# A vision tower on one core: new slots, orders and banks for a planned pipeline, with filler matmuls

## The chip, the cores and the metric

The kernel runs on one core of one Trainium2 chip. Its time is the device time in microseconds (us) of one execution. The engines are PE (TensorE), DVE (VectorE), ACT (ScalarE), POOL (GpSimd) and SP (SyncE, which issues all DMAs here). Each takes its instructions strictly in program order.

## What is computed

64 images (3x224x224) are cut into 196 tokens of 256 numbers each. Then come four blocks, each with a residual and a layer norm:

```python
h = tok(x)                                    # 16x16 patches @ W + b
h = ln(h + attn0(h)); h = ln(h + ffn0(h))     # level 0
h = ln(h + attn1(h)); h = ln(h + ffn1(h))     # level 1
# attn0: xz = h @ in_proj; xb = silu(conv4(xb)); dt, B, C = split(xb @ x_proj)
#   dt = softplus(dt * dt_w + dt_b); dA = exp(dt * A)        (512 x 16 states)
#   state[t] = dA[t] * state[t-1] + (xb * dt)[t] * B[t]      (scan over tokens)
#   y = sum_n state * C + xb * D; out = (ln(y) * silu(z)) @ out_w
# ffn0: r = sigmoid(mix(h) @ W_r); k = relu(mix(h) @ W_k)^2; r * (k @ W_v)
# attn1: 8 heads, leaky scores, softmax over 196 tokens, * gamma + x
# ffn1: 8 experts, top 2 by a softmax gate, weighted sum of x @ We + be
```

Everything is float32.

## The kernel before

One image takes 16 **groups** in the scan of attn0: 4 channel blocks of 128 by 4 sets of 4 states. The program is cut into **slots**; one slot holds one group, and an image has 16. Every other block of an image has a slot number of its own in the tables at the top (`AT_...`), counted from the image's first scan: from -41 (load the image) to 89 (store its result). So in each of the 16 slots (slot number modulo 16) the engines work on up to nine images at once. `schedule` writes the program out image by image; `step` in each engine's part goes through the slots, and within a slot the order of its `for s, q in at(...)` lines is the order of that engine's work. Engines meet only through semaphores.

For group g of an image:

- POOL, `inputs` (L464): X = u * B, in slot g-1. X is a ring of six tiles.
- ACT, `decay` (L873): four exponentials into a ring of two dA tiles, in slot g-1.
- DVE, `scan_group` (L1070): two scans over X, in slot g.
- POOL, `times_c` (L474): X = X * C, in slot g+1.
- PE, `sum_states` (L579): transposes X and adds up the states in PSUM bank YB, in slot g+2. ACT empties YB once in four groups (`drain_y`, L880).

The work around the scan that the prediction speaks of:

- `softplus` (L854, L859, L862) in four pieces on ACT: relu, abs, exp, log. The log needs another activation table, so it is followed by a reload ahead of the next `decay`. POOL then adds (dt, L451) and multiplies (u, L454) for the next image: `make_u`.
- `inverse_std` (L479 to L486): four or two small POOL instructions per layer norm ("att", "y", "ffn", "out", "moe"), which wait for `moments` (L1075, L1079) on DVE.
- ffn0: `token_major(.., "r")` and `mix_keys` on PE (L619, L627), `drain_rk` on ACT (rs L915, ka L920), the square on POOL (ka L504), then `token_major(.., "v")`. The first of these needs a PSUM bank that DVE's `add_residual` (accT, L1195) gives free.
- `project_out` on PE (L600, L603) after POOL's y3 product (L511); then `queries_keys` (L636), `drain_qk` (L927, L929), and DVE's `gate_x` (L1055) after ACT's `tanh_of_x` (L828).
- ffn1: DVE's `scale_pair` (hg, L1186) makes one of four pairs of experts at a time in a ring of two tiles; PE's `expert_pair` (L699) uses it.
- attn1: `scores`, `drain_scores` (L937), `row_max` (L1117), `probs` (L944), `turn_probs` (L658), `drain_pT` (L952), `mix_values` (L671), `attended` (L1129 to L1134). Before, the slots of the drains, maxima and exponentials are tied to those of the matmuls: `AT_SCORES[n] + 1`, `+ 2`, `+ 3`, `AT_TURN_P[n] + 1`, `AT_AV[n] + 1`.

Three PSUM banks (G0, G1, G2) are shared by tables of uses; a use can start when the use before it in the same bank has been drained.

Of the kernel before, what the change touches and what calls it, by code (L numbers as in the profile page):

```python
# [11 lines left out]
P = 128  # L12
# [5 lines left out]
T = SIDE * SIDE  # L18
BLK = 2
# [38 lines left out]
AT_LOAD = -41  # L58
AT_PATCH = (-30, -30, -26,)
# [13 lines left out]
AT_SOFT = (-9, -9, -8, -8,)  # L73
AT_U = -7
AT_B = (-2, -4, -1, 0,)
AT_C = (-1, -2, 0, 0,)
AT_Y_OUT = (6, 9, 12, 17,)
# [3 lines left out]
AT_Y_STD = 20  # L81
# [3 lines left out]
AT_Y3 = 24  # L85
# [5 lines left out]
AT_H1T_OUT = 30  # L91
# [22 lines left out]
AT_H3T_OUT = 64  # L114
# [3 lines left out]
AT_TOP2 = 68  # L118
# [66 lines left out]
def vit_tower(nc, x, w_tok, b_tok, w_in, conv_w, conv_b, w_xproj, a_log, d_par, dt_w, dt_b, w_out, ln_g, ln_b,  # L185
              w_r, w_k, w_v, mu_r, mu_k, w_qk, b_q, b_k, w_vv, b_v, gamma, w_g, b_g, w_e, b_e,
              ident, q_mask, k_mask, rank_of, proj, gates, out):
    with ExitStack() as ctx:
# [183 lines left out]
        def _(sp):  # L372
# [40 lines left out]
            def step(b, par):  # L413
                for g in range(GROUPS):
                    def at(slot):
                        return live(b, par, g, slot)

                    for s, q in at(AT_LOAD):
                        load(s)
                    for s, q in at(AT_GATE_STORE):  # L420
                        store_gates(s)
# [24 lines left out]
        def _(pool):  # L446
# [41 lines left out]
            def step(b, par):  # L488
                for g in range(GROUPS):
# [857 lines left out]
```

## Time and profile before

| what | value |
|---|---|
| median of 3 runs | 5539.83 us |
| lowest, highest | 5514.9, 5540.97 us |
| the profiled execution | 5522.53 us, span of the core 5520.7 us |
| busy: PE, DVE, ACT, POOL | 86%, 68%, 71%, 81% of the span |
| mean granted TensorE clock | 0.917 of full speed |

The span begins with the loads of the weights and the first images, whose first scan starts after about 77 us, and ends with 185 us in which the last images pass through the blocks behind the scan. Between them lie 63 steps from image to image, nearly all alike. Busy shares are means over a whole step: in one slot an engine may be the one that all wait for, and in the next have nothing to do.

### The profile page before, as it was taken

Reading aid. Unit: us, or ns where it says so; the run is one execution under the profiler, and the core shown is the slowest. Engines: PE = TensorE matmul, PEld = TensorE weight load, DVE = VectorE, ACT = ScalarE, POOL = GpSimd, SP = SyncE. Lnnn points to the kernel's source line nnn. Section 1 sums busy time; section 2 is a strip of 40 time slices with the busy share of each in tenths; the row PEclk is TensorE's granted clock in tenths of the full one; section 3 lists DMA queues with packets and bytes.
Section 4 is the critical chain, followed back from the end, with each engine's and each line's share of the span. In section 5 each row is a group of like instructions: output and inputs, shape, how many; then the busy total and the mean of one; then the engine's idle time right before and its main releaser. Section 6 shows DMA issues by size and latency. Waiting matters only on the chain.

```text
span 5520.7 us, 91938 instructions
## 1 busy us (share of the span) xinstructions
PE 4738.8 (86%) x31488; PEld 4137.2 (75%) x31488; DVE 3737.4 (68%) x7504; ACT 3925.5 (71%) x9282; POOL 4455.6 (81%) x3336
## 2 busy tenths in 40 slices
PE   4788889888888888888888888888888888888887
PEld 3677777777777777777777777777777777777776
DVE  3667666667677667667677677676776776766663
ACT  4777777777777777776777777777776777776752
POOL 4988888888888888888888888888888888887860
PEclk7889989999999999999999999999999999999887
DMA  4222222222222222222222222222222222222110
GB/s 105 63 47 60 68 55 56 71 50 61 67 54 61 66 56 61 61 60 61 55 67 61 55 64 64 55 62 66 55 62 66 55 58 69 55 57 70 41 39 24
DMA packets 730609, 328.76 MB, mean 60 GB/s; under 512 B 631543, under 2 KB 655393, under 8 KB 729889
## 3 DMA queue, kind: packets, MB, share of 16 engines
q1 hardware_dynamic: 730144, 322.89, 24.0%
q8 instruction: 252, 4.13, 0.3%
q14 instruction: 213, 1.74, 0.1%
HBM read 307.88 MB, written 14.90 MB: 58 GB/s over the span
## 4 chain that ended last, share of the span: by engine, by line
DVE 35%; PE 26%; ACT 26%; issue 9%; POOL 3%; SPq 1%; DMA 0%; DVEq 0%; ACTq 0%; POOLq 0%
DVE X L1070 14%; PE G L699 8%; ACT dA L873 6%; PE YB L579 4%; DVE xbs L1047 3%; DVE nmx L1117 3%; PE SB L658 3%; PE G L619 2%; PE G L671 2%; ACT dt L854 2%; ACT soft L854 2%; ACT y L888 2%; DVE hg L1186 2%; ACT pT L952 2%; ACT pr L937 2%
## 5 line engine op out<-in xcount | busy, mean ns | idle before, releaser
L1070 DVE TENSOR_TENSOR_SCAN X<-dA,X 128x392 f32<-128x392 f32 x2048 | 1875.7, 958 | 1203.7 <-ACT dA L873 1165.0
L474 POOL TENSOR_TENSOR X<-X,Cb 128x784 f32<-128x784 f32 x1024 | 1894.7, 1850 | 4.2 <-DVE X L1070 4.2
L464 POOL TENSOR_TENSOR X<-u,Bb 128x784 f32<-128x784 f32 x1024 | 1895.3, 1851 | 2.2 <-DMA Bb<-proj_rows 2.1
L873 ACT ACTIVATE dA<-dt,negA 128x195 f32<-128x195 f32 x4096 | 1524.0, 417 | 303.3 <-DVE X L1070 263.5
L579 PE MATMUL YB<-idn,X 128*98 128x128 f32 x8192 | 1152.7, 289 | 33.3 <-POOL X L474 33.3
L579 PEld LDWEIGHTS YB<-idn,X 128*98 128x98 f32 x8192 | 973.6, 136 | 138.4 <-POOL X L474 116.8
L699 PE MATMUL G<-hg,we 128*128 128x196 f32 x4096 | 771.9, 348 | 49.8 <-DVE hg L1186 49.6
L699 PEld LDWEIGHTS G<-hg,we 128*128 128x128 f32 x4096 | 730.3, 203 | 61.1 <-issue 58.4
L556 PE MATMUL SB<-hT,win 128*128 128x196 f32 x2048 | 454.9, 386 | 184.2 <-ACT pT L952 170.6
L556 PEld LDWEIGHTS SB<-hT,win 128*128 128x128 f32 x2048 | 415.4, 226 | 214.0 <-ACT hT L808 192.3
L671 PE MATMUL G<-vs,pT 98*98 98x33 f32 x4096 | 428.0, 262 | 130.7 <-DVE att L1134 113.0
L671 PEld LDWEIGHTS G<-vs,pT 98*98 98x98 f32 x4096 | 419.2, 181 | 160.2 <-issue 158.0
L880 ACT ACTIVATE ysb<-YB 98x256 f32<-98x256 f32 x256 | 96.5, 377 | 584.0 <-PE YB L579 540.8
L944 ACT ACTIVATE pr<-pr,nmx 98x196 f32<-98x196 f32 x1024 | 385.0, 450 | 106.6 <-DVE nmx L1117 96.1
L648 PE MATMUL SB<-km,qm 32*98 32x392 f32 x1024 | 255.5, 540 | 169.3 <-DVE xbs L1055 159.5
L1047 DVE SCALAR_TENSOR_TENSOR xbs<-SB,cw,xbs 128x195 f32<-128x195 f32 (+2 forms) x768 | 268.1, 411 | 174.4 <-ACT xbs L817 170.4
L479 POOL TENSOR_TENSOR veps_att<-mv_att,epsc 98x2 f32<-98x2 f32 x64 | 12.5, 195 | 459.0 <-DVE mv_att L1079 459.0
L451 POOL TENSOR_TENSOR dt<-dt,soft 128x784 f32<-128x784 f32 x64 | 117.7, 1839 | 261.6 <-ACT soft L862 261.6
L952 ACT ACTIVATE pT<-SB 98x784 f32<-98x784 f32 x256 | 209.7, 819 | 150.5 <-PE SB L658 114.1
L1186 DVE TENSOR_TENSOR hg<-G,Gb 128x784 f32<-128x784 f32 x256 | 240.5, 961 | 101.7 <-PE G L699 98.3
L547 PE MATMUL G<-patT,wtok 128*128 128x196 f32 x1536 | 275.9, 337 | 11.6 <-ACT patT L799 11.1
L658 PE MATMUL SB<-idn,pr 98*98 98x98 f32 x2048 | 260.8, 279 | 20.3 <-DVE zs L1060 8.7
(147 smaller groups left out, 7379.4 us busy)
## 6 DMA issues: line engine op xcount, KB each, us to landing
Bb<-proj_rows SPq DMA_DIRECT2D x256, 392.0 KB, 4.4
Cb<-proj_rows SPq DMA_DIRECT2D x256, 392.0 KB, 3.8
Gb<-gate_rows SPq DMA_DIRECT2D x64, 784.0 KB, 4.7
px<-in_x SPq DMA_DIRECT2D x1024, 36.8 KB
out<-ob SPq DMA_DIRECT2D x64, 196.0 KB
dtin<-proj_rows SPq DMA_DIRECT2D x64, 98.0 KB, 2.8
we<-in_w_e SPq DMA_DIRECT2D x1, 2048.0 KB
proj_rows<-pj SPq DMA_DIRECT2D x64, 25.3 KB
```

The lines of the kernel that those rows point to most:

```text
L464: tt(X[(GROUPS * s + g) % RING][:], u[q % 2][:, c:c + 1, :].broadcast_to([P, NG, T]), Bb[:, NG * ng:NG * (ng + 1), :], ALU.mult).then_inc( ...
L474: tt(t[:], t[:], Cb[:, n0:n0 + NG, :], ALU.mult).then_inc(prod_ready, 1)
L556: last = mm(o[:, j // 2, (j % 2) * T:(j % 2 + 1) * T], lhsT=win[:, k, m * P:(m + 1) * P], rhs=src[:, k, :], start=(k == 0), stop=(k == DC ...
L579: last = mm(YB[0:TB, k * P:(k + 1) * P], lhsT=X[(GROUPS * s + g) % RING][:, j, k * TB:(k + 1) * TB], rhs=idn[:], is_transpose=True, start= ...
L658: last = nc.tensor.transpose(o[0:TB, j // 2, at:at + TB], pr[(UNITS * s + n) % PRING][:, j, k * TB:(k + 1) * TB], idn[:TB, :TB])
L671: last = mm(o[0:TB, j * (DV + 1):(j + 1) * (DV + 1)], lhsT=pT[:, j // 2, at:at + TB], rhs=vs[q % 2][:, k, h0 + j, :], start=(k == 0), stop ...
L699: last = mm(o[:, m * T:(m + 1) * T], lhsT=we[:, k, at:at + P], rhs=hg[p % GRING][:, e, k, :], start=(p == 0 and e == 0 and k == 0 and m == 0),
L873: last = go(dA[i % DRING][:, j, 1:T], dt_[q % 2][:, c, 1:T], ACT.Exp, scale=negA[:, c, n:n + 1])
L944: last = go(pr[i % PRING][:, j, :], pr[i % PRING][:, j, :], ACT.Exp, bias=nmx[i % PRING][:, j:j + 1])
L1047: last = v.scalar_tensor_tensor(out=xbs[:, c, k:], in0=S.tile[:, c // 2, at:at + T - k], scalar=cw[:, c, TAPS - 1 - k:TAPS - k], in1=xbs[: ...
L1070: v.tensor_tensor_scan(t, dA[i % DRING].rearrange("p n t -> p (n t)"), t, 0.0, ALU.mult, ALU.add).then_inc(scan_done, 1)
L1186: v.tensor_tensor(hg[p % GRING][:], h, w, ALU.mult).then_inc(hg_ready, 1)
```

## The change

- Every block that was tied to another has a table entry now: `AT_PR`, `AT_MAX`, `AT_PROBS`, `AT_PT`, `AT_MEET` for attn1 and `AT_IN`, `AT_TIMES`, `AT_DECAY` for the scan. Some keep the old distance, others do not.
- The four pieces of softplus have slots -11, -9, -9, -9 in place of -9, -9, -8, -8.
- `keep_busy(n)` puts n matmuls (98 x 196) on PE whose result nobody reads, in five places per image: 4, 4, 4, 3 and 2 of them in slots 5, 8, 9, 12 and 13. They wait for nothing.
- Most slots shift by one or two; some blocks change the order within their slot on each engine; patch0 moves from bank G0 to bank G2.

The instructions are otherwise the same, in number and size.

```diff
+AT_WARM = (5, 8, 9, 12, 13,)
+WARM = (4, 4, 4, 3, 2,)
-AT_LOAD = -41
+AT_LOAD = -39
-AT_PATCH = (-30, -30, -26,)
+AT_PATCH = (-30, -29, -26,)
-AT_SOFT = (-9, -9, -8, -8,)
+AT_SOFT = (-11, -9, -9, -9,)
-AT_B = (-2, -4, -1, 0,)
-AT_C = (-1, -2, 0, 0,)
-AT_Y_OUT = (6, 9, 12, 17,)
+AT_B = (-4, -4, -1, -1,)
+AT_C = (-1, -3, 3, 0,)
+AT_Y_OUT = (6, 10, 12, 17,)
-AT_Y_STD = 20
+AT_Y_STD = 21
-AT_Y3 = 24
+AT_Y3 = 25
-AT_H1T_OUT = 30
+AT_H1T_OUT = 28
-AT_KSQ = 34
+AT_KSQ = 33
-AT_FFN_STATS = 37
+AT_FFN_STATS = 36
-AT_FFN_NORM = 39
+AT_FFN_NORM = 40
-AT_TURN_P = (49, 51, 53, 56,)
+AT_TURN_P = (49, 51, 53, 55,)
+AT_PR = (45, 46, 49, 51,)
+AT_MAX = (46, 48, 50, 52,)
+AT_PROBS = (47, 49, 51, 53,)
+AT_PT = (50, 52, 54, 57,)
+AT_MEET = (53, 54, 57, 60,)
-AT_ATT = 61
-AT_ATT_NORM = 60
+AT_ATT = 60
+AT_ATT_NORM = 62
-AT_TOP2 = 68
+AT_TOP2 = 70
-AT_SCALE = (76, 76, 77, 78,)
-AT_PAIR = (77, 77, 78, 80,)
+AT_SCALE = (76, 76, 76, 77,)
+AT_PAIR = (77, 77, 78, 79,)
...
@@ POOL's step: the order now
-                    for k in range(GROUPS):
-                        for s, q in at(k - 1):
-                            inputs(s, q, k)
-                    for n, slot in (("y", AT_Y_STD), ("out", AT_OUT_STD), ("ffn", AT_FFN_STD), ("att", AT_ATT_STD),
-                                    ("moe", AT_MOE_STD)):
+                    for s, q in at(AT_OUT_STD):
+                        inverse_std(s, "out")
+                    for s, q in at(AT_Y_STD):
+                        inverse_std(s, "y")
                     for s, q in at(AT_KSQ):
...
+                    for s, q in at(AT_ATT_STD):
+                        inverse_std(s, "att")
+                    for s, q in at(AT_U):
+                        make_u(s, q)
+                    for s, q in at(AT_FFN_STD):
+                        inverse_std(s, "ffn")
                     for k in range(GROUPS):
-                        for s, q in at(k + 1):
-                            times_c(s, k)
+                        for s, q in at(k + AT_IN):
+                            inputs(s, q, k)
                     for s, q in at(AT_Y3):
...
+                    for k in range(GROUPS):
+                        for s, q in at(k + AT_TIMES):
+                            times_c(s, k)
@@ PE
+            def keep_busy(n):
+                for _ in range(n):
+                    mm(YB[0:TB, BLK * P:BLK * P + T], lhsT=idn[:, 0:TB], rhs=win[:, 0, 0:T], start=False, stop=False,
+                       skip_group_check=True)
```

Where instructions move, three places show it. X0 to X5 are the tiles of the ring; a row with `Bb` is `inputs`, one with `Cb` is `times_c`.

POOL around the square of ffn0 (`ka`), before:

```order
L474 TENSOR_TENSOR X5<-X5,Cb 128x784
L464 TENSOR_TENSOR X2<-u1,Bb 128x784
L474 TENSOR_TENSOR X0<-X0,Cb 128x784
L464 TENSOR_TENSOR X3<-u1,Bb 128x784
L504 TENSOR_TENSOR ka<-ka 128x392
L474 TENSOR_TENSOR X1<-X1,Cb 128x784
L464 TENSOR_TENSOR X4<-u1,Bb 128x784
```

And now:

```order
L484 TENSOR_TENSOR X4<-X4,Cb 128x784
L474 TENSOR_TENSOR X1<-u1,Bb 128x784
L484 TENSOR_TENSOR X5<-X5,Cb 128x784
L509 TENSOR_TENSOR ka<-ka 128x392
L474 TENSOR_TENSOR X2<-u1,Bb 128x784
L484 TENSOR_TENSOR X0<-X0,Cb 128x784
L474 TENSOR_TENSOR X3<-u1,Bb 128x784
```

The square stood behind the product that makes X3; it stands two such products earlier now, ahead of the one that makes X2.

POOL around softplus (`dt`, `u`) and `y3`, before:

```order
L479 TENSOR_TENSOR veps_moe<-mv_moe,epsc 98x2
L483 TENSOR_TENSOR rstd_moe<-veps_moe,mhalf 98x2
L474 TENSOR_TENSOR X3<-X3,Cb 128x784
L511 TENSOR_TENSOR y3<-y3,zs 128x784
L464 TENSOR_TENSOR X0<-u0,Bb 128x784
L451 TENSOR_TENSOR dt1<-dt1,soft 128x784
L454 TENSOR_TENSOR u1<-dt1,xbs 128x784
L474 TENSOR_TENSOR X4<-X4,Cb 128x784
L464 TENSOR_TENSOR X1<-u0,Bb 128x784
```

And now:

```order
L489 TENSOR_TENSOR veps_moe<-mv_moe,epsc 98x2
L493 TENSOR_TENSOR rstd_moe<-veps_moe,mhalf 98x2
L474 TENSOR_TENSOR X1<-u1,Bb 128x784
L484 TENSOR_TENSOR X5<-X5,Cb 128x784
L461 TENSOR_TENSOR dt0<-dt0,soft 128x784
L464 TENSOR_TENSOR u0<-dt0,xbs 128x784
L474 TENSOR_TENSOR X2<-u1,Bb 128x784
L524 TENSOR_TENSOR y3<-y3,zs 128x784
L484 TENSOR_TENSOR X0<-X0,Cb 128x784
```

`dt` and `u` stand one `inputs` earlier in their image; `y3` stood ahead of them and stands behind them now.

DVE around the pairs of experts (`hg`), before (the scan of X0 is group 12 of its image):

```order
L1084 TENSOR_SCALAR h1<-G1,mv_out,rstd_out 98x256 x2
L1070 SCALAR_TENSOR_TENSOR X0<-dA,X0 128x392 x2
L1186 TENSOR_TENSOR hg0<-G0,Gb 128x784
L1186 TENSOR_TENSOR hg1<-G0,Gb 128x784
L1070 SCALAR_TENSOR_TENSOR X1<-dA,X1 128x392 x2
L1186 TENSOR_TENSOR hg0<-G0,Gb 128x784
L1075 BN_STATS stat_att<-att 98x6 x2
L1079 BN_AGGR mv_att<-stat_att 98x2 x2
L1070 SCALAR_TENSOR_TENSOR X2<-dA,X2 128x392 x2
L1186 TENSOR_TENSOR hg1<-G0,Gb 128x784
```

And now:

```order
L1105 SCALAR_TENSOR_TENSOR X0<-dA,X0 128x392 x2
L1164 RECIPROCAL rg<-G2 98x4
L1166 TENSOR_TENSOR G2<-G2,rg 98x4x32
L1169 SCALAR_TENSOR_TENSOR att<-h21,G2 98x128
L1221 TENSOR_TENSOR hg0<-G0,Gb 128x784
L1221 TENSOR_TENSOR hg1<-G0,Gb 128x784
L1221 TENSOR_TENSOR hg0<-G0,Gb 128x784
L1110 BN_STATS stat_att<-att 98x6 x2
L1114 BN_AGGR mv_att<-stat_att 98x2 x2
L1105 SCALAR_TENSOR_TENSOR X1<-dA,X1 128x392 x2
L1221 TENSOR_TENSOR hg1<-G0,Gb 128x784
L1105 SCALAR_TENSOR_TENSOR X2<-dA,X2 128x392 x2
```

`attended` of the last unit (rg, G2, att) stands behind the scan of group 12 now, and three of the four `hg` and the moments of "att" ahead of the scan of group 13; the norm `h1` has moved ahead of this piece.

## Rows read from the trace of the kernel before

**Rows 1.** The page: busy time by engine, and granted clock in 40 slices.

```profile
PE 4738.8 (86%) x31488; PEld 4137.2 (75%) x31488; DVE 3737.4 (68%) x7504; ACT 3925.5 (71%) x9282; POOL 4455.6 (81%) x3336
...
PEclk7889989999999999999999999999999999999887
```

**Rows 2.** The timeline (start, duration, instruction, idle before) of POOL: `dt` 40 images apart.

```profile
890.40 1.84 POOL L451 TENSOR_TENSOR dt<-dt,soft 128x784 f32<-128x784 f32 x1 [3.50 <-ACT soft L862]
...
4225.12 1.84 POOL L451 TENSOR_TENSOR dt<-dt,soft 128x784 f32<-128x784 f32 x1 [3.45 <-ACT soft L862]
```

**Rows 3.** Windows: length; busy PE, PEld, DVE, ACT, POOL; clock; DMA share; GB/s.

```profile
1683.10:1764.10 81.00, 69.77 (x494) 60.52 (x492) 58.24 (x118) 61.09 (x146) 69.64 (x53) 0.98 0.26 64
2016.30:2098.90 82.60, 72.42 (x494) 63.54 (x492) 58.23 (x117) 61.13 (x146) 69.63 (x53) 0.94 0.25 63
...
2042.00:2047.00 5.00, 4.92 (x32) 4.74 (x31) 4.12 (x9) 3.58 (x7) 4.53 (x6) 0.54 0.01 2
```

**Rows 4.** The waits of POOL: us in total, times, longest.

```profile
POOL veps_att L479 <- DVE mv_att L1079: 459.0, 64, 20.0
...
POOL dt L451 <- ACT soft L862: 261.6, 61, 65.4
...
POOL veps_ffn L479 <- DVE mv_ffn L1079: 135.6, 62, 8.2
...
POOL veps_out L479 <- DVE mv_out L1079: 38.5, 61, 8.4
```

**Rows 5.** Instruction groups: count, busy us, mean ns, idle before.

```profile
L464 POOL TENSOR_TENSOR X<-u,Bb 128x784 f32<-128x784 f32 x1024 | 1895.3, 1851 | 2.2 <-DMA Bb<-proj_rows 2.1
L873 ACT ACTIVATE dA<-dt,negA 128x195 f32<-128x195 f32 x4096 | 1524.0, 417 | 303.3 <-DVE X L1070 263.5
```

**Rows 6.** The timeline of POOL in the image that starts at 2016.29.

```profile
2023.48 0.84 POOL L504 TENSOR_TENSOR ka<-ka 128x392 f32<-128x392 f32 x1 [0.30 <-ACT ka L920]
...
2086.28 0.19 POOL L479 TENSOR_TENSOR veps_att<-mv_att,epsc 98x2 f32<-98x2 f32 x1 [6.02 <-DVE mv_att L1079]
```

**Rows 7.** The timeline of DVE in the same image.

```profile
2016.29 1.84 DVE L1070 TENSOR_TENSOR_SCAN X<-dA,X 128x392 f32<-128x392 f32 x2 [1.27 <-ACT dA L873]
...
2046.38 1.84 DVE L1070 TENSOR_TENSOR_SCAN X<-dA,X 128x392 f32<-128x392 f32 x2 [0.81 <-ACT dA L873]
...
2073.60 0.15 DVE L1129 RECIPROCAL rg<-G 98x4 f32<-98x4 f32 x1
...
2074.33 1.39 DVE L1047 SCALAR_TENSOR_TENSOR xbs<-SB,cw,xbs 128x193 f32<-128x193 f32 x4
...
2077.50 0.99 DVE L1084 TENSOR_SCALAR h<-G,mv_out,rstd_out 98x256 f32<-98x256 f32 x2
2078.40 1.83 DVE L1070 TENSOR_TENSOR_SCAN X<-dA,X 128x392 f32<-128x392 f32 x2
...
2092.29 0.95 DVE L1186 TENSOR_TENSOR hg<-G,Gb 128x784 f32<-128x784 f32 x1
...
2098.93 1.84 DVE L1070 TENSOR_TENSOR_SCAN X<-dA,X 128x392 f32<-128x392 f32 x2 [1.27 <-ACT dA L873]
```

**Rows 8.** The timeline of ACT there.

```profile
2054.21 1.88 ACT L854 ACTIVATE soft<-dtin,dtb,dtw 128x196 f32<-128x196 f32 x4
...
2059.75 0.86 ACT L862 ACTIVATE soft<-soft 128x784 f32<-128x784 f32 x1
...
2075.75 0.83 ACT L828 ACTIVATE SB<-xbs 128x784 f32<-128x784 f32 x1 [0.76 <-DVE xbs L1047]
...
2087.98 1.08 ACT L907 ACTIVATE h<-att,shift_att,rstd_att 98x256 f32<-98x256 f32 x2
```

**Rows 9.** The timeline of PE there.

```profile
2066.50 1.89 PE L600 MATMUL G<-wout,y 128*98 128x256 f32 x8
...
2081.24 5.54 PE L699 MATMUL G<-hg,we 128*128 128x196 f32 x32 [1.26 <-DVE hg L1186]
```

**Rows 10.** The page: a DMA issue, KB each, us to landing.

```profile
Bb<-proj_rows SPq DMA_DIRECT2D x256, 392.0 KB, 4.4
```

More of the change, by code:

```diff
@@ L721, in at @@
                         return live(b, par, g, slot)
+                    for s, q in at(AT_WARM[0]):
+                        keep_busy(WARM[0])
+                    for s, q in at(AT_WARM[4]):
+                        keep_busy(WARM[4])
+                    for s, q in at(AT_H3T):
+                        pe.wait_ge(normed["att"], s + 1)
+                        turn(s, "h3T", h3)
+                    for s, q in at(AT_WARM[1]):
+                        keep_busy(WARM[1])
+                    for s, q in at(AT_WARM[2]):
+                        keep_busy(WARM[2])
                     for s, q in at(AT_H3T2):
@@ L726, in step @@
                         turn_y(s)
+                    for s, q in at(AT_WS):
+                        turn_gates(s)
+                    for s, q in at(AT_GATE):
+                        gate(s, q)
+                    for s, q in at(AT_WARM[3]):
+                        keep_busy(WARM[3])
+                    for p in range(PAIRS):
+                        for s, q in at(AT_PAIR[p]):
+                            expert_pair(s, p)
+                    for s, q in at(AT_MOE_T):
+                        turn_moe(s)
+                    for s, q in at(AT_EMBED):
+                        embed(s)
                     for s, q in at(AT_V):
@@ L751, in step @@
                             scores(s, n)
+                    for n in range(UNITS):
                         for s, q in at(AT_TURN_P[n]):
                             turn_probs(s, n)
+                    for s, q in at(AT_RK):
+                        pe.wait_ge(mix_step, 4 * (s + 1))
+                        token_major(s, "r", xr, wr)
+                        mix_keys(s)
+                    for n in range(UNITS):
                         for s, q in at(AT_AV[n]):
                             mix_values(s, q, n)
-                    for s, q in at(AT_WS):
-                        turn_gates(s)
+                    for s, q in at(AT_H1T):
+                        pe.wait_ge(where["out"].drained, where["out"].count("out", s))
+                        turn(s, "h1T", h1)
+                    for s, q in at(AT_QK):
+                        queries_keys(s)
                     for k in range(GROUPS):
@@ L765, in step @@
                         project_in(s, hT[q], "xb", 0)
-                    for s, q in at(AT_RK):
-                        pe.wait_ge(mix_step, 4 * (s + 1))
-                        token_major(s, "r", xr, wr)
-                        mix_keys(s)
+                    for s, q in at(AT_XPROJ):
+                        xproj(s)
                     for s, q in at(AT_OUT):
                         project_out(s, q)
-                    for s, q in at(AT_H1T):
-                        pe.wait_ge(where["out"].drained, where["out"].count("out", s))
-                        turn(s, "h1T", h1)
                     for s, q in at(AT_H2T):
@@ L960, in step @@
                         normalise(s, "ffn", rs, h2[q % 2])
-                    for s, q in at(AT_GATE_EXP):
-                        act.wait_ge(gate_step, GSTEPS * s + GIN)
-                        o = where["gate"].tile[0:TB, 0:BLK * EXPERTS]
-                        go(o, o, ACT.Exp).then_inc(gate_exp, 1)
                     for s, q in at(AT_H2T_OUT):
@@ L1224, in step @@
                             scale_pair(s, p)
-                    for s, q in at(AT_MIX):
-                        token_mix(s)
+                    for n in range(UNITS):
+                        for s, q in at(AT_MAX[n]):
+                            row_max(s, n)
                     for t, which in AT_TAPS.items():
```

149 lines of the change are left out of this document (69 added, 80 removed).

## The prediction

> **What bounds the kernel now.** I read the page first. No engine is full: PE 86%, POOL 81%, DVE and ACT about 70%, the same in all slices between head and tail, with the granted clock at 9 tenths in all but the ends [rows 1]. So one step from image to image tells nearly all. Two `dt` products of POOL 40 images apart are 3334.7 us apart, a **step of 83.4 us** [rows 2]. Sixty such steps fill the middle.
>
> Two images of the windows give the parts of a step [rows 3]. POOL is busy 69.6 us in either; an image at clock 0.98 takes 81.0 us and one at 0.94 takes 82.6 us. POOL's work is fixed (of the 52 instructions per image, 35 are long, of 1.85 us [rows 5], with starts 1.80 us apart), so a step is POOL's work plus POOL's waits. The list of waits names them, per image: the moments of "att" 459.0/64 = 7.2 us, softplus 3.1 us (without the 65.4 us at the start), "ffn" 2.1 us, "out" 0.6 us [rows 4]. In the image that starts at 2016.29 the wait for "att" is 6.02 us and that for the square of ffn0 0.30 us [rows 6], for softplus and "ffn" about their means. These make some 12.2 us there, so that POOL's work with its small gaps is 82.6 - 12.2 = **70.4 us**. What the reader should see: the step can't be under 70.4 us, and a change helps only if it shortens these waits without making new ones. I measure times of the new step from its first scan (S = 0), and call T the scan of group 12.
>
> **The change, wait by wait.**
>
> *"ffn", 2.1 us: gone.* The moments move from slot 37 to 36, on DVE right behind the sum that they read, and POOL asks in slot 38 as before. One more slot is over 4 us, more than the wait.
>
> *Softplus, 3.1 us: gone, by a thin margin.* The first piece moves out of the crowded slots 7 and 8 into slot 5, the other three run together in slot 7. In the old image the log starts 2059.75 - 2016.29 = 43.5 us after the first scan [rows 7, 8]. Out of its way go relu (1.8 us, like abs [rows 8]), decay 9 (four of 417 ns, 1.5 us with their overlap [rows 5]) and two drains, the norm of "ffn" above all (some 1 us, like that of "att" [rows 8]). Against it, top 2, fifteen small DVE instructions, moves from slot 3, where it held scan 4 up, to slot 6: scan 7 comes at some 31.9 us in place of 2046.38 - 2016.29 = 30.1 us [rows 7], and decay 8 must wait for its first half, 32.9 us. From there decay, abs, exp, table and log take 6.4 us: ready at 39.3 us. POOL gets there at 7.2 us (the square, below) plus 33.3 us of its own work, 40.5 us. Only 1.2 us lies between; that is the first rival.
>
> *The square of ffn0: 0.3 becomes 2.2 us.* The square starts 7.2 us after the first scan, since the chain before it (scan, maximum, residual, r, k, relu) keeps its order [rows 6, 7]. But it stands ahead of the product for X2 now, not behind that for X3. POOL arrives earlier and waits, and scan 2 comes at 9.9 us, not 7.9 us. From here POOL works without a stop: 41 us of work, and `y3`, now behind `dt`, `u` and one more product, is done at 48.2 us.
>
> *From y3 to scan 12.* Before, `project_out` starts at 2066.50 and scan 12 at 2078.40, 11.9 us [rows 7, 9]. In this chain the last value product stands ahead of `queries_keys` now (+1.4, the 1.5 us of such a group less overlap), the norm of "out" has left it (-1.0 [rows 7]), and tanh no longer waits 0.76 us for the third tap [rows 8]. T = 48.2 + 11.9 + 1.4 - 1.0 - 0.8 = 59.7, say 59.8 us. It was 2078.40 - 2016.29 = 62.1 us: **2.3 us gained**.
>
> *"att" stays, about 6 us.* Before, POOL had the moments 2086.28 - 2078.40 = 7.9 us after scan 12 [rows 6, 7]: they stand behind an `hg` that needs the first pair of experts on PE. They still do; `attended` (2073.60 to 2074.33, 0.7 us [rows 7]) joins ahead of the pairs, so 8.6 us. POOL is free at 7.2 + (70.4 - 1.3 - 14.4) + 0.7 for "out" = 62.6 us and waits till 68.4 us: 5.9 us. Moving the moments ahead of scan 13 gains nothing, since the same `hg` stands ahead of them.
>
> *From scan 12 to the next image.* Before: 2098.93 - 2078.40 = 20.5 us [rows 7]. `attended` adds 0.7, the norm of "att" (1.08 us, between the emptied bank and the decay of group 14) moves out (-1.1) [rows 8], one `hg` leaves slot 14 (-0.95) [rows 7]. The mask of old tokens (h1T and its two scalings) goes from slot 14 to ACT's long wait in slot 12, the second unit's drain from slot 15 to 14; both are then hidden. 19.3 us, and the next scan 0 at 79.2 us: **1.2 us gained**. POOL alone, 1.3 for "att" and five products of 1.8 behind 68.4, is at 78.8 us, so it all but sets this too. The two ways agree: 70.4 + 5.9 + 0.7 + 2.2 = 79.2 us.
>
> *Filler matmuls.* 17 per image, each in two passes, at 5.54/32 = 0.17 us a pass [rows 9]: 5.9 us of PE. At nothing, if PE has the time. PE's work at full clock is 69.8 us [rows 3], with them 75.7 of 79.2 us. Slot 5's four stand where PE waited for `attended`; slots 8 and 9's (2.8 us) ahead of an `xb` projection that must be done by 49 us and is by 46.5; slots 12 and 13's (1.7 us) in the waits for the tanh gate and the first `hg`. What they buy is clock: behind that wait PE ran at a mean of 0.54, that is mostly at 1.2 GHz, in a stretch where it was busy 4.92 of 5 us [rows 3]. The mean image costs 83.4 - 81.0 = 2.4 us more than the one at clock 0.98. My chain was read from a 2016.29 image whose slow stretch hardly touches it, so I count no gain on top, and add 0.3 us for clock that still falls: **79.5 us**. The Trainium skill (TensorE: Matmul & The Clock Gate, PE-mode transpose) says that transposes don't count as PE being busy. That speaks against the change: between the value product of slot 5 and the embedding of slot 7 PE has only transposes and waits, so by it the clock falls there all the same, and fillers of slot 5 buy little. The slow stretch of the old trace, full of transposes, agrees.
>
> *Loads.* B and C rows (392 KB, 4.4 us to land [rows 10]) are asked for earlier or need a later product; the burst of four comes at the turn of the image and lands within some 9 us, against uses from 8 us on (C0, X2). The image's load moves behind the gates' store, with over 40 us to spare. Nothing.
>
> **The sum.** Per step 83.4 - 79.5 = 3.9 us, over 60 steps 234 us. Head and tail have no fillers and the same chains: 0, give or take 6. The profiled execution was 5522.5 us (span 5520.7), so 5289 us; the median of the runs is 17 us above it, so 5306 us.
>
> **Rivals.**
> 1. *ACT stays the bound in slots 5 to 10.* Against me: three pieces and a table load in slot 7 put decay 9 at 42 us, 2 us later than before, and the 1.2 us margin of `dt` is small. If 2 us of the old 3.1 us wait remain, the step is 81.5 us: 5540 - 60 x 1.9 = 5426 us. For me: ACT's load in those slots is unchanged, only its start is earlier. Chance 0.15.
> 2. *The clock isn't held.* By the rule above, and with less slack on PE than before, slow stretches reach the projections or the pairs and cost the mean 2.4 us again: step 81.9 us, 5450 us. The skill's rule gives about this. Chance 0.1.
> 3. *Slower: POOL's waits first.* Small waiting instructions and the square stand ahead of `inputs` now, so whatever is late holds the next product and thereby the scan. If the later chain from scan 2 on keeps its old length (83.4 - 7.9 = 75.5 us), because what was shortened wasn't on it, scan 2 at 9.9 us makes the step 85.4 us: 5540 + 60 x 2 = 5660 us. It decides as soon as less than 2 us come back between scan 2 and the end; I count 6.2. Chance 0.08.
> 4. *More than I see.* The wait for "att" shrinks, as scan 12 may come earlier against POOL: step 77.5 us, 5185 us. Chance 0.05.
> 5. *Waits only change places,* step 83 us, 5516 us. Chance 0.04.
>
> **The numbers.** My forecast has 0.58, with its own range 5240 to 5370 us. The range that holds 8 in 10 takes in rivals 1 and part of 2 above, and half of 4 below: 5210 to 5445 us. A measurement of this kernel tells 0.5% (28 us) from no change. Faster by more than that: 0.58 + 0.15 + 0.1 + 0.05 = 0.88. Within: 0.04. Slower: 0.08.
>
> **What would show it.** Right: `dt` products 79 to 80 us apart; POOL's waits for "ffn" and softplus near nothing, for "att" still 5 to 7 us per image, for the square about 2 us; scan 2 9.9 us and scan 12 60 us behind the first scan; PE near 92% busy. Wrong: POOL waiting over 1 us for softplus (rival 1), a clock under 0.93 with slow stretches in slots 9 to 13 (rival 2), or scan 3 to 12 spaced as before behind a later scan 2 (rival 3).

## The result and the profile after

The changed kernel takes **5291.61 us** (median of 4 runs, 5288.81 to 5295.57) where the kernel before took 5540.4 us in runs beside it (5514.9 to 5551.01): a ratio of 0.956 [0.9525, 0.9591]. The forecast was 5306 us. One run further down (6153.03 us at a granted clock of 0.745, of the kernel with the moments of "att" moved) was in a slower state of the chip and is left out of its median.

The page of the changed kernel (busy time by engine; granted clock in 40 slices), against [rows 1]:

```profile
span 5291.6 us, 96290 instructions
...
PE 4820.6 (91%) x33664; PEld 4234.3 (80%) x33664; DVE 3739.1 (71%) x7504; ACT 3911.0 (74%) x9282; POOL 4452.7 (84%) x3336
...
PEclk8899999999999999999999999999999999999986
...
L548 PE MATMUL YB<-win,idn 128*98 128x196 f32 x2176 | 424.1, 335 | 0.0
```

POOL, DVE and ACT do the work that they did. PE has 82 us more: the fillers (L548, 34 matmul instructions per image for the 17 calls, each counted once per pass) are 424 us of it, 6.6 us per image, so PE's own work takes 342 us less than before, and no instruction of it was dropped. That is a first sign of the clock. The windows of 4000 us in the middle say it outright (length; busy PE, PEld, DVE, ACT, POOL; clock; DMA share; GB/s); of the kernel before:

```profile
1000.00:5000.00 4000.00, 3498.09 (x23603) 3059.90 (x23602) 2796.04 (x5615) 2939.03 (x6960) 3342.09 (x2496) 0.93 0.25 61
```

and of the changed kernel, with one image below it:

```profile
1000.00:5000.00 4000.00, 3739.09 (x26549) 3291.53 (x26548) 2944.45 (x5917) 3079.87 (x7323) 3520.58 (x2634) 0.99 0.26 63
```

```profile
1930.26:2008.97 78.71, 73.18 (x528) 64.28 (x527) 58.31 (x118) 60.94 (x147) 69.51 (x53) 1.00 0.26 64
```

The waits of POOL in the changed kernel (us in total, times, longest), against [rows 4]:

```profile
POOL veps_att L489 <- DVE mv_att L1114: 435.0, 64, 23.6
...
POOL ka L509 <- ACT ka L954: 125.6, 62, 13.2
...
POOL dt L461 <- ACT soft L896: 69.4, 4, 65.1
...
POOL veps_out L489 <- DVE mv_out L1114: 51.2, 62, 10.4
```

"ffn" has two waits left in the whole execution (9.5 us), and softplus hardly more than the one of the start (65.1 of 69.4 us): these are the two waits that the slots were to remove. The square stands at (125.6 - 13.2)/61 = 1.8 us per image. "att" stands at (435.0 - 23.6)/63 = 6.7 us.

The timeline of POOL in the changed kernel: the image whose first scan is at 1930.26 (the row of L524 is `y3`), and `dt` 40 images apart, against [rows 2, 6].

```profile
862.91 1.87 POOL L461 TENSOR_TENSOR dt<-dt,soft 128x784 f32<-128x784 f32 x1
...
1937.45 0.84 POOL L509 TENSOR_TENSOR ka<-ka 128x392 f32<-128x392 f32 x1 [1.82 <-ACT ka L954]
...
1970.80 1.85 POOL L461 TENSOR_TENSOR dt<-dt,soft 128x784 f32<-128x784 f32 x1
...
1976.34 1.85 POOL L524 TENSOR_TENSOR y<-y,zs 128x784 f32<-128x784 f32 x1
...
1998.49 0.20 POOL L489 TENSOR_TENSOR veps_att<-mv_att,epsc 98x2 f32<-98x2 f32 x1 [6.06 <-DVE mv_att L1114]
...
4028.76 1.85 POOL L461 TENSOR_TENSOR dt<-dt,soft 128x784 f32<-128x784 f32 x1
```

The step is (4028.76 - 862.91)/40 = **79.15 us**, where it was 83.4 us; sixty times the difference of 4.2 us is 253 us. The two profiled spans differ by 5520.7 - 5291.6 = 229 us only. The rest lies behind the last scan, in the windows from there to the end; of the kernel before:

```profile
5336.10:5520.70 184.60, 150.00 (x868) 131.44 (x866) 77.19 (x219) 56.47 (x120) 18.03 (x40) 0.78 0.08 24
```

and of the changed kernel:

```profile
5084.10:5291.60 207.50, 156.06 (x874) 134.42 (x872) 77.13 (x218) 56.53 (x121) 20.97 (x42) 0.74 0.06 21
```

The **tail** takes 207.5 us where it took 184.6: 23 us were given back there, 17 of them as idle time of PE and 6 as busy time. In both, the clock is low in it. The head kept its length: the first `dt` starts at 66.0 us where it started at 66.3.

The timeline of DVE in the same image, scans 0, 2, 7 and 12 and the next image's scan 0, against [rows 7]:

```profile
1930.26 1.84 DVE L1105 TENSOR_TENSOR_SCAN X<-dA,X 128x392 f32<-128x392 f32 x2 [1.14 <-POOL X L474]
...
1940.14 1.84 DVE L1105 TENSOR_TENSOR_SCAN X<-dA,X 128x392 f32<-128x392 f32 x2 [4.12 <-POOL X L474]
...
1962.22 1.82 DVE L1105 TENSOR_TENSOR_SCAN X<-dA,X 128x392 f32<-128x392 f32 x2
...
1989.88 1.83 DVE L1105 TENSOR_TENSOR_SCAN X<-dA,X 128x392 f32<-128x392 f32 x2
...
2008.97 1.84 DVE L1105 TENSOR_TENSOR_SCAN X<-dA,X 128x392 f32<-128x392 f32 x2 [1.12 <-POOL X L474]
```

Scan 2 stands at 9.9 us, scan 7 at 32.0, scan 12 at 59.6 and the next scan 0 at 78.7. ACT's log, the last piece of softplus, in the same image:

```profile
1968.86 0.86 ACT L896 ACTIVATE soft<-soft 128x784 f32<-128x784 f32 x1
```

It ends 39.5 us after the first scan, and POOL's `dt` starts at 40.5 without a wait: the margin is 1.1 us.

### The profile page after: what moved, and what is told of

The parts are those of the page before. It is cut to its first block and busy times, and to the rows that moved or that the text cites. A ratio compares the mean times of both kernels' runs of the same rounds, so it can differ in the third digit from the quotient of the medians.

```text
span 5291.6 us, 96290 instructions
## 1 busy us (share of the span) xinstructions
PE 4820.6 (91%) x33664; PEld 4234.3 (80%) x33664; DVE 3739.1 (71%) x7504; ACT 3911.0 (74%) x9282; POOL 4452.7 (84%) x3336
## 5 line engine op out<-in xcount | busy, mean ns | idle before, releaser
L601 PE MATMUL YB<-idn,X 128*98 128x128 f32 x8192 | 1106.7, 281 | 25.6 <-POOL X L484 25.4
L601 PEld LDWEIGHTS YB<-idn,X 128*98 128x98 f32 x8192 | 931.3, 132 | 62.9 <-POOL X L484 33.9
L721 PE MATMUL G<-hg,we 128*128 128x196 f32 x4096 | 727.8, 334 | 27.1 <-DVE hg L1221 27.1
L721 PEld LDWEIGHTS G<-hg,we 128*128 128x128 f32 x4096 | 694.9, 194 | 47.4 <-issue 40.8
L578 PE MATMUL SB<-hT,win 128*128 128x196 f32 x2048 | 375.3, 337 | 58.0 <-ACT pT L986 55.8
L548 PE MATMUL YB<-win,idn 128*98 128x196 f32 x2176 | 424.1, 335 | 0.0
L693 PE MATMUL G<-vs,pT 98*98 98x33 f32 x4096 | 397.8, 253 | 21.0 <-DVE ob L1119 9.2
L578 PEld LDWEIGHTS SB<-hT,win 128*128 128x128 f32 x2048 | 340.1, 192 | 84.5 <-issue 66.2
L489 POOL TENSOR_TENSOR veps_att<-mv_att,epsc 98x2 f32<-98x2 f32 x64 | 12.6, 197 | 435.0 <-DVE mv_att L1114 435.0
L548 PEld LDWEIGHTS YB<-win,idn 128*98 128x98 f32 x2176 | 350.1, 169 | 3.2
L680 PE MATMUL SB<-idn,pr 98*98 98x98 f32 x2048 | 219.7, 251 | 66.2 <-DVE zs L1095 62.5
```

What stands on the lines that cost most here:

```text
L548: mm(YB[0:TB, BLK * P:BLK * P + T], lhsT=idn[:, 0:TB], rhs=win[:, 0, 0:T], start=False, stop=False, skip_group_check=True)
L578: last = mm(o[:, j // 2, (j % 2) * T:(j % 2 + 1) * T], lhsT=win[:, k, m * P:(m + 1) * P], rhs=src[:, k, :], start=(k == 0), stop=(k == DC ...
L601: last = mm(YB[0:TB, k * P:(k + 1) * P], lhsT=X[(GROUPS * s + g) % RING][:, j, k * TB:(k + 1) * TB], rhs=idn[:], is_transpose=True, start= ...
L693: last = mm(o[0:TB, j * (DV + 1):(j + 1) * (DV + 1)], lhsT=pT[:, j // 2, at:at + TB], rhs=vs[q % 2][:, k, h0 + j, :], start=(k == 0), stop ...
L721: last = mm(o[:, m * T:(m + 1) * T], lhsT=we[:, k, at:at + P], rhs=hg[p % GRING][:, e, k, :], start=(p == 0 and e == 0 and k == 0 and m == 0),
```

## The experiments

Two readings of the result had to be told apart. The first is the prediction's: the slots shorten the chain of an image, and the fillers add little. The second: the slots need the full clock, and it is the fillers that give it. Each run below has its time as a ratio to the kernel before on the same chip, with the 95% interval, from three rounds. The runs were made on three chips, on which the kernel before took 5535.67, 5539.64 and 5530.45 us; so a difference of times from two chips is good to some 10 us. Where a slot is named in which the clock falls, it is counted in the 40 images from the eleventh on, by DVE's scans.

**Fillers out.** Slots, banks and orders as changed.

```diff
-WARM = (4, 4, 4, 3, 2,)
+WARM = (0, 0, 0, 0, 0,)
```

> The changed kernel with its five filler counts at 0. Theory: the new slots alone give the chain of 79.2 us per image, and the fillers save the clock's part: the old mean image cost 2.4 us more than one at clock 0.98, the new one 0.5 us more than its best (79.15 against 78.7 us). So without fillers the clock falls back to some 0.92 and the step to about 81.2 us: 5292 + 60 x 2.1 = 5415 us. Rival 1, slots alone: the slow stretches fall where PE has slack now, step 79.5 us, under 5320 us. Rival 2, fillers carry nearly all: over 5480 us.

5462.71 us, 0.9873 [0.9852, 0.9893], 48 us over the expectation; the middle, in the windows view:

```profile
1000.00:5000.00 4000.00, 3515.94 (x24010) 3096.18 (x24010) 2843.93 (x5705) 2982.86 (x7086) 3396.02 (x2542) 0.94 0.25 61
```

The fillers are worth 171 us (175 by the two ratios). Without them nearly every image is 82 us long and has two stretches at half clock at the same places: a short one that begins in slot 6 (2022.2 to 2025.6 in the image whose first scan is at 1994.5) and a longer one in slot 9 (2039.3 to 2046.1). The first costs next to nothing: `y3` is done 47.9 us after the first scan, as with fillers. The timeline of PE around the second, and in slot 12:

```profile
2036.49 1.04 PE L601 MATMUL YB<-idn,X 128*98 128x128 f32 x8
...
2040.03 5.57 PE L578 MATMUL SB<-hT,win 128*128 128x196 f32 x16 [2.50 <-ACT pT L986]
2045.39 2.26 PE L622 MATMUL G<-wout,y 128*98 128x256 f32 x8
...
2057.54 0.90 PE L670 MATMUL SB<-km,qm 32*98 32x392 f32 x4 [2.65 <-DVE xbs L1090]
```

`y3` in the timeline of POOL there:

```profile
2040.56 1.84 POOL L524 TENSOR_TENSOR y<-y,zs 128x784 f32<-128x784 f32 x1
```

The timeline of PE in the changed kernel, at the same place of its image:

```profile
1972.07 1.49 PE L548 MATMUL YB<-win,idn 128*98 128x196 f32 x8
1973.40 1.04 PE L601 MATMUL YB<-idn,X 128*98 128x128 f32 x8
...
1975.57 2.89 PE L578 MATMUL SB<-hT,win 128*128 128x196 f32 x16 [1.14 <-ACT pT L986]
...
1978.30 1.91 PE L622 MATMUL G<-wout,y 128*98 128x256 f32 x8
```

The xb projection takes 5.57 us in place of 2.89: half the clock. It comes behind a wait of 2.50 us for pT; with fillers in slots 8 and 9 the wait is 1.14 us and the clock stays. xb stands right ahead of `project_out` on PE: in the kernel without fillers `y3` is ready at 2042.40, and `project_out` starts at 2045.39, when xb is through. So the delay of xb goes straight into `project_out`, scan 12 and the step. The length of a wait alone doesn't decide: the one of 2.65 us in slot 12 of the same image has the full clock behind it. The tail is 208 us long here too: it is the slots that lengthened it, not the fillers.

**Fillers in the kernel before.** The same five calls, no other change.

```diff
+AT_WARM = (5, 8, 9, 12, 13,)
+WARM = (4, 4, 4, 3, 2,)
...
+            def keep_busy(n):
...
+                    mm(YB[0:TB, BLK * P:BLK * P + T], lhsT=idn[:, 0:TB], rhs=win[:, 0, 0:T], start=False, stop=False,
```

> The kernel before with the same fillers (4, 4, 4, 3, 2 in slots 5, 8, 9, 12, 13 at the same places of PE's order). Theory: they hold the clock near its best image of 81.0 us at no cost of PE time: 5540 - 60 x 2.1 = 5415 us, clock 0.96 or more. Rival 1: the slots before have their PE waits elsewhere, so the 5.9 us of fillers stand partly on the path: no change or slower, 5540 us or more. Rival 2: clock rises but the slow stretches were hidden: 5500 us.

5484.27 us, 0.9905 [0.9884, 0.9926], 69 us over the expectation, at a clock of 0.96 where the kernel before has 0.93. So fillers alone bring 51 us, slots alone 73 us (the run before), and both together 249 us. The parts need each other: in the old slots the clock still falls in slots 5 or 6 (24 times in the 40 images) and 11 or 12 (39 times), and POOL still waits 208.4 us for softplus and 134.8 us for "ffn" (before 261.6 and 135.6 [rows 4]), and 482.9 us for "att" in place of 459.0.

**Fillers of some slots only.**

```diff
-WARM = (4, 4, 4, 3, 2,)
+WARM = (0, 4, 4, 0, 0,)
```

> The changed kernel with only the fillers of slots 8 and 9 (4 and 4). Without any filler the trace shows the xb projection and project_out in slots 9 and 10 at half clock in every image, behind a wait of PE, and slot 10 takes 10.2 us in place of 7.65. Theory: these eight fillers alone undo that, some 2.6 of the 2.9 us per step: 5310 us (5295 to 5335). Rival, every filler counts alike (8 of 17): 5463 - 171 x 8/17 = 5382 us.

5440.74 us, 0.9817 [0.9799, 0.9834]: wrong by 130 us. The xb projection is healed, and then, in the timeline of PE of this kernel:

```profile
2029.77 2.82 PE L578 MATMUL SB<-hT,win 128*128 128x196 f32 x16
...
2044.20 0.90 PE L670 MATMUL SB<-km,qm 32*98 32x392 f32 x4 [2.64 <-DVE xbs L1090]
...
2047.56 8.13 PE L721 MATMUL G<-hg,we 128*128 128x196 f32 x32 [0.76 <-DVE hg L1221]
```

a half-clock stretch has appeared further on. Behind the wait for the tanh gate (2.64 us, in slot 12, where no filler stands) the first two pairs of experts take 8.13 us in place of 5.54 [rows 9]. These hold up the `hg` ahead of the moments of "att": POOL waits 570.6 us for them in all, 459.2 us without any filler. The stretch in slot 6 has grown too, and the clock of the middle is lower than without fillers, 0.92 against 0.94. The windows around the two stretches of this kernel (first scan at 1983.7):

```profile
2011.90:2018.60 6.70, 6.61 (x33) 5.81 (x31) 6.00 (x25) 6.16 (x17) 6.62 (x6) 0.50 0.02 5
2046.00:2052.70 6.70, 5.94 (x21) 5.54 (x19) 2.26 (x4) 3.05 (x9) 0.00 (x0) 0.50 0.07 25
```

Healing one stretch brought 22 us. Yet the wait of slot 12 was as long without fillers (2.65 us) and harmless there; why it lets the clock fall here isn't shown.

The counterpart, `WARM = (4, 0, 0, 0, 0,)`:

> The changed kernel with only the four fillers of slot 5. Theory: what follows them up to the embedding is transposes and waits, in which other engines set the pace anyway (the rule on transposes), so 5440 to 5465 us, as without fillers. Rival, they hold the clock through slots 6 to 10: 5350 us or less.

5453.72 us, 0.9842 [0.9823, 0.9861]. Slot 5's four alone are worth 9 us, no more than the chips differ, and xb takes 5.57 us as before. The time fell into the expected range, but the reason given there, the rule on transposes, isn't borne out below. By themselves the two sets make 22 and 9 us (31 and 17 by the ratios); all five make 171 us. With no fillers, with those of slots 8 and 9 and with those of slot 5, most images take 81.9 us, whichever place has the half clock; that they agree so closely stays unexplained.

**What fillers cost where the cover is gone.**

```diff
-WARM = (4, 4, 4, 3, 2,)
+WARM = (4, 8, 8, 3, 2,)
```

> The changed kernel with eight fillers each in slots 8 and 9 in place of four. Prices the cover: PE waits 1.14 us ahead of xb in slot 9 now, the eight more take 2.8 us, so xb and project_out come 1.6 to 1.7 us later and so does every image: 5292 + 60 x 1.65 = 5390 us. Rival 1, PE has more slack than the trace shows (y3 and DVE set the pace): under 5310 us. Rival 2, PE is the bound and all of it counts: 5292 + 60 x 2.8 = 5460 us.

5382.02 us, 0.9714 [0.9697, 0.9731]: 90 us more than the changed kernel, for 8 more calls of two passes, 16 x 0.17 = 2.7 us of PE per image; the mean step is 80.7 us, so 1.6 of the 2.7 us show. "At nothing" holds for the 17 as placed, and not for twice as many in slots 8 and 9, which lie ahead of xb and, through it, of `project_out`.

**Transposes as fillers.** Each filler gives way to three transposes of the same operands.

```diff
-                for _ in range(n):
-                    mm(YB[0:TB, BLK * P:BLK * P + T], lhsT=idn[:, 0:TB], rhs=win[:, 0, 0:T], start=False, stop=False,
+                for _ in range(3 * n):
+                    mm(YB[0:TB, BLK * P:BLK * P + P], lhsT=win[:, 0, 0:TB], rhs=idn[:], is_transpose=True, start=False, stop=False,
```

> The changed kernel with each filler matmul replaced by three transposes of 98 x 128 by the identity into the same place, so that PE is busy about as long in the same slots, with the kind of work that the state sums do. If only matmuls that multiply hold the clock (the rule on transposes), the clock falls to 0.92 and the time to that without fillers, 5450 to 5470 us. Rival, whatever keeps PE busy holds it: 5292 us, clock 0.965.

5298.59 us, 0.9581 [0.9563, 0.9598], and the window:

```profile
1000.00:5000.00 4000.00, 3740.33 (x27376) 3307.82 (x27375) 2940.66 (x5911) 3075.09 (x7314) 3514.62 (x2632) 0.98 0.26 63
```

As fillers, transposes hold the clock as the matmuls do, with nearly the same time of PE (421.8 us against 424.1). The work around them is the same in both.

**The old slots of softplus** in the new kernel.

```diff
-AT_SOFT = (-11, -9, -9, -9,)
+AT_SOFT = (-9, -9, -8, -8,)
```

> The changed kernel with softplus back in slots -9, -9, -8, -8. Theory (the margin of 1.2 us that dt had): relu, a decay and the norm of ffn stand ahead of the log again, it ends at about 44.3 us after the first scan while POOL is there at 40.5 us; POOL waits 3.8 us per image, y3, project_out and all behind come as much later: step 82.5 us, 5292 + 60 x 3.8 = 5520 us. Rival: ACT does the same work in slots 5 to 10 either way, so at most 1 us per step: under 5350 us.

5652.29 us, 1.0213 [1.019, 1.0235]: slower than the kernel before, and 132 us over the expectation. The waits of POOL:

```profile
POOL veps_att L489 <- DVE mv_att L1114: 494.9, 64, 21.6
...
POOL dt L461 <- ACT soft L896: 309.4, 64, 70.8
```

and a `dt` in its timeline:

```profile
1935.77 1.85 POOL L461 TENSOR_TENSOR dt<-dt,soft 128x784 f32<-128x784 f32 x1 [3.77 <-ACT soft L896]
```

Images at full clock take 82.5 us, 3.8 us over the best of the changed kernel, as expected. Most take 85.2 us: in 36 of the 40 images the clock falls in slots 10 and 12 in spite of the fillers. That POOL's wait is passed on to PE there is a reading, not shown by an edit. This one table entry is worth 361 us, more than the whole change gained.

**The square behind the product for X2.**

```diff
-                    for s, q in at(AT_KSQ):
-                        pool.wait_ge(where["k"].drained, where["k"].count("k", s))
-                        tt(ka[:], ka[:], ka[:], ALU.mult).then_inc(ksq_ready, 1)
...
+                    for s, q in at(AT_KSQ):
+                        pool.wait_ge(where["k"].drained, where["k"].count("k", s))
+                        tt(ka[:], ka[:], ka[:], ALU.mult).then_inc(ksq_ready, 1)
```

> The changed kernel with POOL's square of ffn0 behind the product of its slot, as it was in the kernel before, no longer ahead. POOL then makes X2 in what was a wait of 1.82 us for relu, and scan 2 comes at 7.9 us in place of 9.9 us. Account of POOL's waits (as in the prediction): a wait of 1.8 us less per step, 5292 - 60 x 1.8 = 5184 us. Rival, chains: from slot 4 on ACT's chain (tanh of z after PE's z, decay 6, pT, y, softplus, pT of the last unit, xb) ties with POOL's and keeps its time, so project_out starts 0.2 us earlier at most and POOL waits elsewhere: 5280 to 5292 us.

5283.19 us, 0.9543 [0.9524, 0.9562]. POOL's waits in this kernel:

```profile
POOL veps_att L489 <- DVE mv_att L1114: 448.1, 64, 23.4
...
POOL veps_out L489 <- DVE mv_out L1114: 101.2, 64, 10.0
POOL dt L461 <- ACT soft L896: 90.1, 54, 67.5
...
POOL ka L520 <- ACT ka L954: 18.6, 4, 13.2
```

107 us of waits for the square went, and 84 us came back: 13 for "att", 50 for "out", 21 for softplus. Of the 1.7 us per image that POOL no longer waits, some 0.1 us is left in the mean step (79.0 us), and 8 us in the time, within the noise. At full clock it is more, 78.2 us in place of 78.7; the middle has a clock of 0.98 here where the changed kernel has 0.99. Why not all of it: `y3` and xb in such an image (first scan at 1770.12), POOL and PE:

```profile
1814.70 1.84 POOL L524 TENSOR_TENSOR y<-y,zs 128x784 f32<-128x784 f32 x1
```

```profile
1814.95 2.89 PE L578 MATMUL SB<-hT,win 128*128 128x196 f32 x16 [0.85 <-ACT pT L986]
1817.68 1.89 PE L622 MATMUL G<-wout,y 128*98 128x256 f32 x8
```

`y3` is done 46.4 us after the first scan, 1.5 us earlier than in the changed kernel. `project_out` starts at 47.6, 0.5 us earlier, because PE has xb in hand till then, and xb waited for ACT's pT.

**The moments of "att" one `hg` earlier.** On DVE, in `expert` work of slot 12:

```diff
+                        if p == GRING:
+                            for s, q in at(AT_ATT):
+                                dve.wait_ge(where["AV3"].drained, where["AV3"].count("AV3", s))
+                                moments(s, "att", lambda k: att[:, k, :])
...
-                    for s, q in at(AT_ATT):
-                        dve.wait_ge(where["AV3"].drained, where["AV3"].count("AV3", s))
-                        moments(s, "att", lambda k: att[:, k, :])
```

> The changed kernel with the moments of att on DVE between the second and third hg, where DVE waits 2.19 us for the first pair of experts, no longer behind the third. POOL gets them 2.7 us earlier, so its largest wait falls from 6.06 to some 3.4 us per image (435 us in all to about 260). Chains: scan 14 waits for the decay of group 14 behind PE's pairs anyway, so the step changes by 0.1 us at most, 5280 to 5292 us, and POOL waits longer for the square instead. Account of POOL's waits: 5292 - 60 x 2.7 = 5130 us.

5267.98 us, 0.9506 [0.9488, 0.9525], 12 us under the expected range. The waits of POOL:

```profile
POOL ka L509 <- ACT ka L954: 314.7, 62, 16.3
POOL veps_att L489 <- DVE mv_att L1114: 210.7, 64, 17.5
```

The largest wait is halved, 224 us of it gone, and 189 us of them stand at the square now. The best image is 0.2 us shorter (78.5 us). The mean step falls by 0.4 us, from 79.15 to 78.76: some half of the 24 us is clock again. With the square moved too, both edits at once:

> The changed kernel with the moments of att between the second and third hg and the square behind the product of its slot. Apart, these gave steps of 78.5 and 78.2 us at full clock against 78.7. POOL waits for att 2.9 us and no more ahead of scan 2, so it runs ahead. If the steps add: 78.0 us at full clock, and with a clock of 0.97 5292 - 60 x 0.6 = 5256 us. Rival, POOL never was the bound in slots 0 to 4: no better than with the moments moved alone, 5269 us.

5269.66 us, 0.9529 [0.9509, 0.9549]: no better than with the moments alone, with a clock of 0.97 where the moments alone have 0.99. Its images at full clock take 78.0 us. The half clock begins in slot 6 or 7 in most images, and in slot 12 in ten of the 40.

**More fillers beside the earlier moments**, and then everything at once.

```diff
-WARM = (4, 4, 4, 3, 2,)
+WARM = (6, 4, 4, 6, 3,)
```

> The kernel with the moments of att moved, and 6, 4, 4, 6, 3 fillers in place of 4, 4, 4, 3, 2: the additions stand in waits of PE (0.95 us ahead of the third turn of slot 5, 1.65 us ahead of the scores of slot 12, 0.43 us ahead of the pairs). Theory: free of cost, and the mean image (78.76 us) comes near its best (78.5 us): 5255 us, clock 0.98. Rival: the additions aren't covered, the pairs start 0.3 us late: 5290 us.

5260.14 us, 0.9509 [0.9492, 0.9525]. The window in the middle of it:

```profile
1000.00:5000.00 4000.00, 3821.68 (x27334) 3371.38 (x27333) 2967.20 (x5944) 3096.86 (x7366) 3541.42 (x2647) 1.00 0.26 64
```

The images of the middle take 78.5 to 78.9 us, with no half-clock time left: six more fillers cost nothing. They also bring little by themselves: the ratio is that of the moments alone (0.9506), and the mean step is 78.6 us where that kernel has 78.8.

> All three: moments of att moved, square behind its product, 6, 4, 4, 6, 3 fillers. If all that holds alone holds together, 78.0 us per image at a clock of 0.98: 5240 us. Rival: a filler or POOL's new pace brings back a slow stretch, 5265 us or more.

**5235.16 us**, 0.9463 [0.9446, 0.9479], the best of all: 1.0% under the changed kernel by the two ratios (0.9463/0.9558). The moved square, worth nothing beside the moments alone, brings 25 us once the clock is held: images of 78.0 us in place of 78.5.

## Why the prediction was right, and what in it was not

**Right, step by step.** In the image at 1930.26, forecast against trace:

| point | forecast | measured |
|---|---|---|
| scan 2 | 9.9 | 9.9 |
| scan 7 | 31.9 | 32.0 |
| log ready, `dt` starts | 39.3, 40.5 | 39.5, 40.5 |
| `y3` done | 48.2 | 47.9 |
| xb projection done | 46.5 | 48.2 |
| scan 12 | 59.8 | 59.6 |
| wait for "att" | 5.9 | 6.06 |
| next scan 0 | 79.2 | 78.7 |
| step with the clock's 0.3 | 79.5 | 79.15 |

"ffn" and softplus gone, the square 2.2 us (1.8 in this image), "att" kept: all hold. What "ffn" brought by itself wasn't tried. The reason for "att" held too: the first pairs on PE take 5.54 us and the `hg` in front of the moments waits for them. Of "moving the moments ahead of scan 13 gains nothing" the run with them one `hg` earlier shows the limits: what gained there, little as it is, is an `hg` less in front, not the scan.

No point on the walk's own path is off by more than 0.5 us. Small slips of its sums (59.8 + 19.3 is 79.1, not 79.2; 68.4 - 62.6 is 5.8, not 5.9) are within that. PE's 69.8 us of work were those of an image at a clock of 0.98, and the fillers take 6.6 us, not 5.9; in the image at 1930.26 PE is busy for 73.2 us where the forecast had 75.7.

**Wrong beside the path: xb.** It was to be done by 46.5 us, 2.5 us before it would matter. It is done at 48.2, level with `y3` (47.9), and `project_out` starts behind both. In all middle images at full clock this is so. The walk came out right at `project_out` because the two tie; that is luck. It decides what comes after: with `y3` 1.5 us earlier (the moved square) `project_out` gained 0.5 us, and eight more fillers ahead of xb cost 1.6 us a step.

**Wrong, and cancelled: the ends.** "Head and tail ... 0, give or take 6" failed: the head kept its length, the tail grew by 23 us, with and without fillers. The steps brought 19 us more than forecast (253 against 234), so the profiled execution came out at 5293.7 us where the sum had 5289. The 17 us by which the median before stood above its profiled execution have no counterpart after (5291.6 against 5293.7 us). The total is as near as it is by two misses of some 20 us that cancel; the 14 us left over are about those 17. I had walked only the middle and taken the chains of the tail for the same; that they are not is measured, what makes them longer isn't shown.

**Wrong: what the fillers buy.** The step that failed is "I count no gain on top". The argument was that the chain had been read from an image that the half-clock stretch hardly touched, so that the clock could only take something away from it, priced at 0.3 us. The sum came out right and the account of it wrong. A chain read at full clock is a forecast for the new slots *under the condition* that the clock holds, and here the fillers are this condition: without them the step is 82.0 us (2.9 us more, 171 us), because xb, at half clock behind the wait for pT, holds up `project_out`. The right price of the fillers was the difference between 79.2 us and what the new slots give with a half-clock xb and `project_out`.

The old trace had this already. "My chain was read from a 2016.29 image whose slow stretch hardly touches it" was a misreading: that image has a second stretch, over xb. The timeline of PE of the kernel before, and its windows around the two stretches:

```profile
2062.09 4.57 PE L556 MATMUL SB<-hT,win 128*128 128x196 f32 x16 [2.88 <-ACT pT L952]
```

```profile
2042.50:2049.20 6.70, 6.62 (x38) 6.19 (x38) 5.68 (x12) 4.42 (x11) 6.54 (x8) 0.50 0.00 1
2049.30:2062.80 13.50, 10.62 (x89) 10.31 (x88) 5.23 (x9) 13.45 (x29) 9.96 (x8) 1.00 0.65 86
2062.90:2066.30 3.40, 3.40 (x12) 3.40 (x11) 1.84 (x2) 3.19 (x9) 3.40 (x3) 0.50 0.35 131
```

xb takes 4.57 us there where it takes 2.89 at full clock, and `project_out` starts at 2066.50, right behind it, though `y3` was ready at 2055.5. So the wait for pT, the half clock and xb stood ahead of `project_out` before the change as well, and the walk left them out.

**Wrong: the rule on transposes.** All transposes of the old half-clock stretch were taken to agree with the rule of the Trainium skill (TensorE: Matmul & The Clock Gate, PE-mode transpose) that they don't count as PE being busy the same way. The exchanged fillers speak against it: 5298.6 us and a clock of 0.98 with transposes, 5291.6 us and 0.99 with matmuls, 5462.7 us and 0.94 with neither. For this kernel's fp32 transposes of 98x128, as fillers, the rule has no hold, and the measurement decides. The old trace speaks against it too: from 2043.2 to 2049.9 PE ran nothing but transposes, and within that time the clock came back from 0.50 to 1.00 (the windows above). What stood ahead of either stretch was a wait of PE, 1.86 and 2.88 us. Rival 2 rested on the rule, and only its other half, less slack on PE, was a danger: that is the kernel without fillers, at 5463 us where the rival had 5450.

**The other rivals.** Rival 1 (softplus): the margin was 1.2 us on paper and is 1.1 us in the trace, and the run with the old slots of softplus shows what lies beyond it, +3.8 us a step at once and 2.7 us more by the clock. A chance of 0.15 for something so near and so dear was not too much. Rival 3 (the later scan 2 stays): mostly not seen; scan 12 comes 2.5 us earlier than before though scan 2 comes 2 us later. But the moved square, with scan 2 at 7.9 us again, takes 0.5 us off an image at full clock (78.7 to 78.2 here, 78.5 to 78.0 in the last run): so much of the 2 us does stay. Rivals 4 and 5 did not come, though a version near 4's mechanism was found: "att" can shrink, but what is gained moves to the square unless both are moved, and then the step is 78.2 us in the mean of 40 images, not 77.5.

**An account is not a price.** That POOL's work and POOL's waits sum to the step is true of any trace. It names where to look. It did not price an edit: 3.5 us less wait for "att" per image made 0.2 us at full clock, 1.7 us less for the square made 0.5 us. The walks from event to event had 0.1 and 0.2 us at most: too low in both, and far nearer than the accounts of 2.7 and 1.8 us.

What stays open: what in the slots made the tail longer, and why the clock still falls in some images of the changed kernel (in slot 6 in 11 of the 40, in slot 12 in 10; such images take 79 to 81 us) and in others not. The new orders and the bank of patch0 weren't tried one by one. Fillers in slot 6 itself weren't tried: they write into the bank that ACT reads there.

## What to carry to other kernels

Walk one image through the new order with durations from rows, and write beside each chain the clock that it needs; then ask which waits of PE stand ahead of that chain. At each meeting point (here `project_out`) follow every engine that arrives there, not only the one that used to come last. Try fillers in all idle places of PE together: here two places or one of the five brought 22 and 9 us, all five 171. Don't price an edit by the wait that it removes on one engine, but by how much earlier the image's last event comes.

## What the runs showed of the hardware

- As a filler in PE's waits, an fp32 transpose holds the clock as well as an fp32 matmul (5298.6 against 5291.6 us; 0.98 against 0.99; 0.94 without fillers).
- With neither, the clock doesn't wander: it falls at the same two places in nearly every image (82.0 us in the mean), and behind a short PE wait (2.50 us ahead of xb) it costs some 3 us each time. A wait of 1.14 us at the same place, behind fillers, cost nothing. A wait of 2.65 us in slot 12 left the clock full in the kernel without fillers, and one of 2.64 us at the same place had half clock behind it with fillers in slots 8 and 9 alone.
- The last microseconds of half clock can go altogether: with 23 fillers per image and a window at 1.00, the images of the middle take 78.5 to 78.9 us.
